# A four-layer graph network on one core: count matrix in bytes, one transfer and one conversion per panel

## What is computed

```
h = relu(layernorm(x)); x = x + spline(h)      # 8 basis weights per edge, segment mean, batch norm, elu
h = relu(layernorm(x)); x = x + gat(h)         # attention: per-edge score, segment softmax, weighted sum
h = relu(layernorm(x)); x = x + gcn3(h)        # three times: agg[dst] += (h@W)[src] * norm, bias, relu
h = relu(layernorm(x)); x = x + sage(h)        # mean of h[src] by dst, joined with h, times W
```

## Time and profile before

| | us |
|---|---|
| median of three timed runs | 11661.3 |
| span of the profiled execution | 9969.6 |
| spline pass, first gather to last | 137 to 3074 |
| GAT pass, first gather to last | 3342 to 6598 |
| four sum passes, first conversion of each | 6737, 7532, 8341, 9157 |
| end of the span | 9970 |

### The profile page before, as it was taken

The page is one execution under the profiler, slowest core; times in us unless marked ns, Lnnn a source line. Parts: engine busy times, 40 slices in busy tenths (PEclk is TensorE's granted clock), DMA queues, the critical chain, the costliest instruction groups (busy, mean ns, idle before and its releaser), DMA issues. The chain is left out here.

```text
span 9969.6 us, 187303 instructions
## 1 busy us (share of the span) xinstructions
PE 7081.0 (71%) x43252; PEld 6159.0 (62%) x43253; DVE 4282.2 (43%) x10967; ACT 4139.5 (42%) x6139; POOL 6744.4 (68%) x6163
## 2 busy tenths in 40 slices
PE   4998888889896466666667777765666766663666
PEld 3998888889895444555555556654554554552555
DVE  6775555555556533333333444452223223224223
ACT  0111111111111233333333444437886885884886
POOL 3667777777775577777777777756655564663663
PEclk9999899999997678878888888878987887996898
DMA  6931111111111333333333333328987996995996
GB/s 244 406 135 17 16 16 16 16 16 16 16 16 5 65 64 64 64 62 64 63 63 62 64 63 64 63 49 250 286 258 219 279 278 186 287 283 161 282 285 195
DMA packets 926246, 1261.57 MB, mean 127 GB/s; under 512 B 326349, under 2 KB 615420, under 8 KB 926075
## 3 DMA queue, kind: packets, MB, share of 16 engines
q1 hardware_dynamic: 403691, 987.27, 29.7%
q0 software_dynamic: 519824, 272.26, 18.0%
q10 hardware_dynamic: 2560, 0.53, 0.0%
HBM read 1052.87 MB, written 206.66 MB: 126 GB/s over the span
## 5 line engine op out<-in xcount | busy, mean ns | idle before, releaser
L561 POOL DMA_INDIRECT gath<-sum_tab,idx_block x1792 | 1788.1, 998 | 1379.4 <-issue 738.0
L837 PE MATMUL psAB<-one_hot,arena 128*128 128x128 f32 x15680 | 2192.7, 299 | 353.5 <-DVE one_hot L1158 352.8
L837 PEld LDWEIGHTS psAB<-one_hot,arena 128*128 128x128 f32 x15680 | 2070.3, 206 | 375.3 <-issue 375.0
L535 POOL DMA_INDIRECT dense<-count_block,cell_block x1120 | 1872.2, 1672 | 524.4 <-issue 329.2
L945 PE MATMUL psCD<-arena_r 128*128 128x512 f32 x5096 | 1513.6, 445 | 642.9 <-ACT arena_r L746 574.1
L561 POOL DMA_INDIRECT gath<-spline_tab,idx_block x1568 | 1512.0, 964 | 632.5 <-issue 417.0
L561 POOL DMA_INDIRECT gath<-gat_tab,idx_block x1568 | 1534.7, 979 | 485.8 <-issue 353.1
L945 PEld LDWEIGHTS psCD<-arena_r 128*128 128x128 f32 x5096 | 1035.9, 214 | 999.2 <-issue 793.7
L746 ACT ACTIVATE arena_r<-stage 128x1792 fp32r<-128x1792 f16 x728 | 1202.8, 1689 | 406.8 <-PE psCD L945 307.4
L1391 DVE SCALAR_TENSOR_TENSOR one_hot<-iota_row,tile_base,dstf 128x512 fp32r<-128x512 f32 x632 | 476.2, 753 | 2043.8 <-PE psAB L931 1724.3
L746 ACT ACTIVATE arena_r<-hT 128x1792 fp32r<-128x1792 f16 x728 | 1199.7, 1687 | 54.7 <-DMA hT<-dense 49.9
(11 more groups left out here) (248 smaller groups left out, 9534.3 us busy)
## 6 DMA issues: line engine op xcount, KB each, us to landing
stage<-dense SPq DMA_DIRECT2D x728, 448.0 KB
hT<-dense SPq DMA_DIRECT2D x728, 448.0 KB
dense<-stage SPq DMA_DIRECT2D x182, 896.0 KB
arena<-dst_rows SPq DMA_DIRECT2D x392, 256.0 KB
gath<-sum_tab,idx_block POOLq DMA_INDIRECT x1792
gath<-spline_tab,idx_block POOLq DMA_INDIRECT x1568
gath<-gat_tab,idx_block POOLq DMA_INDIRECT x1568
sum_tab<-arena_r SPq DMA_DIRECT2D x28, 896.0 KB, 4.7
```

The source lines that it names most:

```text
L535: nc.gpsimd.indirect_dma_start(out=dense, out_offset=bass.IndirectOffsetOnAxis(ap=cell_block[:, c:c + 1], axis=0), in_=count_block[:, c:c ...
L561: nc.gpsimd.indirect_dma_start(out=dest[:, s, j, :], out_offset=None, in_=table, in_offset=bass.IndirectOffsetOnAxis(ap=idx_block[:, c:c + ...
L837: nc.tensor.matmul(block, z[:, w, j, k * P:(k + 1) * P], oh32[:, j, :], start=(j == 0), stop=(j == J - 1))
```

## The change

The matrix is held in bytes (`u8`). A panel of seven tiles is one transfer of 448 KB and one ScalarE conversion of 3584 elements; seven panel buffers take the place of two pairs of halves: two each in `stage`, `hT` and the end of `arena`, one in `early`, an area that held weights and batch norm sums. SyncE loads panel u once panel u - 7 has been turned. Zeroing takes 91 transfers of 896 KB.

Scatters go 41 to a block and begin one iteration earlier (`S0` = 1); 13 are left for the end of the GAT pass.

A byte holds less, so the sources are counted in the GAT pass: in each of the first 35 iterations, for every group, VectorE compares the high and the low part of the source numbers with 0 to 127 (two bf16 operations of 128x512 into `marks`), TensorE multiplies the two one-hots into a 128x128 count in `psE`, and VectorE takes its maximum once per iteration. If a source occurs more than 60 times in one iteration, the matrix is off. `dense_known` is therefore set at the end of the GAT pass and not in the setup, and a quad's sum is multiplied by the flag. SyncE waits for `dense_known` and `scattered` before it stores the first table.

The fp32r product, the gathers and the order of the rounds stay.

```diff
-    SB = 44
-    S0 = 2
+    SB = 41
+    S0 = 1
     NX = 1
-    NY = 20
+    NY = 13
...
-    HC = UC // 2
+    NP = 7
+    CAP = 120
+    LEAD = 4
...
-    JR, JS = 8, 32
+    JR, JS = 16, 64
...
-    dense = nc.dram_tensor("dense", ((NQ * QROWS + JR) * QC, 1), fp16).ap()
+    dense = nc.dram_tensor("dense", ((NQ * QROWS + JR) * QC, 1), u8).ap()
...
+        arena_panels = arena[:, o:o + UC // 2]
...
+        early = sb("early", [P, UC // 4])
+        w_spline, bn = early[:, 0:4 * F], early[:, 4 * F:8 * F]
...
+        src_hi, src_lo = (hT[:, k * DC // 2:(k + 1) * DC // 2].bitcast(bf16) for k in range(2))
+        iota_b = hT[:, DC:DC + P // 2].bitcast(bf16)
+        most = hT[:, DC + P:DC + P + ID]
+        in_tile = stage[:, 0:DC].bitcast(i32)
+        marks = stage[:, 0:2 * GE].bitcast(bf16).rearrange("p (w k j n) -> p w k j n", w=2, k=2, j=J)
...
-        panel = [a[:, h * HC // 2:(h + 1) * HC // 2].bitcast(fp16) for a in (stage, hT) for h in range(2)]
+        panel = [a[:, h * UC // 4:(h + 1) * UC // 4].bitcast(u8) for a in (stage, hT, arena_panels) for h in range(2)]
+        panel += [early[:, :].bitcast(u8)]
...
-            zeros = stage[:, :].bitcast(fp16)
+            zeros = stage[:, :].bitcast(u8)
             sp.dma_start(dense[NQ * QROWS * QC:(NQ * QROWS + JR) * QC, :].rearrange("(p x) o -> p (x o)", p=P),
                          zeros[:, 0:JS]).then_inc(zeroed, 16)
             for q in range(NQ):
-                for u in range(NU):
-                    sp.dma_start(dense_rows[:, q, u * UC:(u + 1) * UC], zeros).then_inc(zeroed, 16)
+                for u in range(NU // 2):
+                    sp.dma_start(dense_rows[:, q, u * 2 * UC:(u + 1) * 2 * UC], zeros).then_inc(zeroed, 16)
...
-            turned = registers(sp, "sp_turned", 2)
+            turned, need = registers(sp, "sp_turned", 2)
 
             def load_panels():
 
                 with sp.Fori(0, NQ) as q:
                     for u in range(NU):
-                        w = u % 2
-                        if w == 0:
-                            sp.reg_add(turned[0], turned[1], 1)
-                            sp.reg_add(turned[1], turned[1], 2)
-                        for h in range(2):
-                            sp.wait_ge(panel_turned[w], turned[h])
-                            sp.sem_inc(panel_free, 1)
-                            at = u * UC + h * HC
-                            sp.dma_start(panel[2 * w + h].unsqueeze(1),
-                                         dense_rows[:, bass.ds(q, 1), at:at + HC]).then_inc(panel_loaded[2 * w + h], 16)
-
+                        sp.reg_add(need, turned, (u + NP) // 2 + 1 + LEAD - NP)
+                        sp.wait_ge(loaded_edges, 16 * 9)
+                        sp.wait_ge(panel_turned[(u + 1) % 2], need)
+                        sp.dma_start(panel[u % NP].unsqueeze(1),
+                                     dense_rows[:, bass.ds(q, 1), u * UC:(u + 1) * UC]).then_inc(panel_loaded[u % NP], 16)
+                    sp.reg_add(turned, turned, NP)
+
+            sp.wait_ge(dense_known, 1)
+            sp.wait_ge(scattered, 16 + 16 * DP)
             with sp.Fori(0, 3) as layer:
                 store_pieces(layer * NS)
-                sp.wait_ge(scattered, 16 + 16 * DP)
...
                 with act.Fori(0, NQ):
                     for u in range(NU):
-                        w = u % 2
+                        w, b = u % 2, u % NP
+                        if b == 0:
+                            act.reg_add(loaded, loaded, 16)
                         if w == 0:
-                            act.reg_add(loaded, loaded, 16)
                             act.reg_add(free, free, 1)
                         act.wait_ge(loaded_edges, 16 * 9)
                         act.wait_ge(panel_used[w], free)
-                        for h in range(2):
-                            act.wait_ge(panel_loaded[2 * w + h], loaded)
-                            nc.scalar.activation(counts[w][:, h * HC:(h + 1) * HC], panel[2 * w + h], ACT.Copy).then_inc(panel_turned[w], 1)
+                        act.wait_ge(panel_loaded[b], loaded)
+                        nc.scalar.activation(counts[w], panel[b], ACT.Copy).then_inc(panel_turned[w], 1)
...
+            def count_sources(i, s):
+
+                pe.wait_ge(marks_ready, i * S + (s + 1))
+                if s == 0:
+                    pe.wait_ge(most_read, i + 1)
+                for j in range(J):
+                    ins = nc.tensor.matmul(psE[:, 0:P], marks[:, s % 2, 0, j, :], marks[:, s % 2, 1, j, :],
+                                           start=(s == 0 and j == 0), stop=(s == S - 1 and j == J - 1))
+                ins.then_inc(marks_used, 1)
+
             pe.wait_ge(visits_init, 2)
-            with pe.Fori(0, IT) as i:
-                group_bounds(pe, i, regs)
-                for s in range(S):
-                    pe.wait_ge(gathered[s], (i + (GAT * IT + 1)) * (16 * J))
-                    with tiles(pe, regs, s):
-                        gat_visit(s)
+            for first, last, counted in ((0, ID, True), (ID, IT, False)):
+                with pe.Fori(first, last) as i:
+                    group_bounds(pe, i, regs)
+                    for s in range(S):
+                        if counted:
+                            count_sources(i, s)
+                        pe.wait_ge(gathered[s], (i + (GAT * IT + 1)) * (16 * J))
+                        with tiles(pe, regs, s):
+                            gat_visit(s)
             with pe.Fori(0, LAG):
...
+            pe.wait_ge(over_known, 1)
+            nc.tensor.matmul(psC[:, 0:4], ones[:, :], over[:, :], start=True, stop=True).then_inc(over_summed, 1)
 
             pe.reg_mov(visit, 0)
 
             first, _ = dense_range(pe, "pe")
             landed, turned, moved, added, pieces = registers(pe, "pe_sum", 5)
-            pe.reg_mov(turned, 2)
...
+            V.tensor_copy(iota_b, iota_row[:, :])
+            link(V.tensor_scalar(in_tile, srci[:, 0:DC], 7, None, ALU.arith_shift_right))
+            link(V.tensor_copy(src_hi, in_tile))
+            link(V.tensor_scalar(in_tile, srci[:, 0:DC], P - 1, None, ALU.bitwise_and))
+            link(V.tensor_copy(src_lo, in_tile))
...
+            def mark_sources(i, s):
+
+                dve.wait_ge(marks_used, i * S + (s + 1))
+                at = bass.ds(i * (S * J) + s * J, J)
+                numbers = iota_b.unsqueeze(1).to_broadcast([P, J, P])
+                V.tensor_tensor(marks[:, s % 2, 0, :, :], numbers, src_hi[:, at].unsqueeze(2).to_broadcast([P, J, P]), ALU.is_equal)
+                V.tensor_tensor(marks[:, s % 2, 1, :, :], numbers, src_lo[:, at].unsqueeze(2).to_broadcast([P, J, P]),
+                                ALU.is_equal).then_inc(marks_ready, 1)
+
+            def read_most(i):
+
+                dve.wait_ge(marks_used, i * S + (S + 2))
+                V.tensor_reduce(most[:, bass.ds(i, 1)], psE[:, 0:P], AX, ALU.max).then_inc(most_read, 1)
+
+            for first, last, counted in ((0, ID, True), (ID, IT, False)):
+                with dve.Fori(first, last) as i:
+                    group_bounds(dve, i, regs)
+                    for s in range(S):
+                        if counted:
+                            mark_sources(i, s)
+                        dve.wait_ge(bc_ready[s % SD], (i * (S // SD) + (s // SD + 1)) * 16)
+                        with tiles(dve, regs, s) as t:
+                            gat_visit(t, dst_bc[:, s % SD, :])
+                        V.engine_nop().then_inc(bc_free[s % SD], 1)
+                        give_back(s)
+                    if counted:
+                        read_most(i)
...
+            link(V.memset(over[:, :], 0.0))
+            link(V.tensor_reduce(over[:, 0:1], most, AX, ALU.max))
+            V.tensor_scalar(over[:, 0:1], over[:, 0:1], CAP // 2 + 0.5, None, ALU.is_ge).then_inc(over_known, 1)
             link(V.reciprocal(s1[:, :], den[:, :]))
             link(V.tensor_tensor(Av, Av, over_features(s1[:, :]), ALU.mult))
+            dve.wait_ge(over_summed, 1)
+            link(V.tensor_scalar(dense_ok[:, :], psC[:, 0:1], 0.0, dense_ok[:, 0:1], ALU.is_equal, ALU.mult))
+            V.tensor_scalar(dense_i[0:1, 0:1], dense_ok[0:1, :], float(ID), None, ALU.mult)
+            V.tensor_scalar(dense_i[0:1, 1:2], dense_ok[0:1, :], float(DB), None, ALU.mult).then_inc(dense_known, 1)
...
-                V.tensor_tensor(at, at, psE[:, 0:QT * F].rearrange("p (t f) -> p t f", f=F),
-                                ALU.add).then_inc(sum_added, 1)
+                V.scalar_tensor_tensor(at, psE[:, 0:QT * F].rearrange("p (t f) -> p t f", f=F), dense_ok[:, 0:1], at,
+                                       ALU.mult, ALU.add).then_inc(sum_added, 1)
```

54 lines of the change are left out of this document (24 added, 30 removed).

## The result

The changed kernel took 11609.95 us (median of 20 runs, 11570.1 to 11646.7) against 11647.1 us (20 runs, 11602.5 to 11676.6) for the kernel before: ratio 0.9969, 95% interval 0.9958 to 0.998, so 37 us faster. The forecast was 98 us. The sign held, and the time lies in the range, which was wide enough to take in the rivals; the size did not hold, and it turns out to depend on the chip.

A forecast was written before the change was run, and what follows sets the result against it. The prediction took GpSimd to pace scatter blocks and the GAT pass, ScalarE the dense quads. Its terms +63 - 84 + 87 + 2 - 166 = -98 us gave 11563 us from 11661.3; range 11420 to 11720, the forecast's own 11490 to 11630.

The forecast's parts named there:

- What bounds the kernel now: Whole kernel: GpSimd paces blocks with scatters and the GAT pass, TensorE blocks without scatters, ScalarE the dense quads.
- slower throughout by 1.17 times: Whole kernel: alternative reading of the 1691.7 us between span and timed median; the gain would then be 115 us.
- schedule term: Spline and GAT passes: 41 scatters per block, starting one iteration earlier, +63 and -84 us, -21 together.
- Zeroing: Start of the spline pass: 91 transfers instead of 182 gain nothing, since the blocks under zeroing are TensorE-bound.
- Scatters: Spline pass +63 us as two blocks become GpSimd-bound; GAT pass -84 us for three fewer scatters in each of 14 blocks.
- Counting: GAT pass: compares hold back GpSimd instructions that start inside them, 0.31 us for each of 280 groups, +87 us.
- Rival A: GAT pass: compares hold GpSimd far oftener, 0.9 us per group, 252 us, so slower at 11728 us; chance 0.13.
- 2.5 us of slack: GAT pass: some 2.5 us per group while TensorE waits for gathers, taken to hide the count's compares and matmuls.
- Dense quads: Sum passes: one transfer and one conversion per panel save 3.2 us in each of 52 quads, -166 us.
- Rival B: Dense quads: TensorE paces, the conversions' gain returns as waits, sum -7, no change at 11654 us; chance 0.15.
- D: Scatters in both passes: adding bytes costs 0.2 us more each, +213, so slower at 11776 us; chance 0.05.
- E: Outside the span: the 1691.7 us shrink with the matrix, up to half of them, some 10800 us; chance 0.04.

The follow-up runs named there:

- e1: The kernel before, unchanged, profiled a second time at the slow pace: 11660.8 us, ratio 1.0013 to the kernel before.
- e2: The changed kernel without the counting of the sources in the GAT pass: 11504.4 us, ratio 0.9882 to the kernel before.
- e4: The changed kernel without the source count and with the old scatter schedule, leaving bytes, single transfer and single conversion: 11433.8 us, ratio 0.9810.
- g1: The changed kernel, unaltered, timed on a chip where the kernel before takes 9967.8 us: 9731.9 us, ratio 0.9763.
- h1: The changed kernel with one counting product per group instead of four, where the kernel before takes 11,661 us: 11580.1 us, ratio 0.9934.
- h2: The changed kernel with a quarter of the compares and all counting products, where the kernel before takes 11,661 us: 11585.7 us, ratio 0.9932.
- e7: The changed kernel with the old scatter schedule and each panel's conversion cut in two halves, at the fast pace: 9814.0 us, ratio 0.9842.
- g4: The changed kernel with the scatter schedule of the kernel before, where the latter takes 9967.8 us: 9763.9 us, ratio 0.9799.
- e3: The changed kernel with the scatter schedule of the kernel before and the count kept, at 11,642 us: 11511.3 us, ratio 0.9876.
- f3: The changed kernel with the source count run in one iteration of 35, where the kernel before takes 11,221 us: 11089.0 us, ratio 0.9891.
- f1: The changed kernel, unaltered, on a chip where the kernel before takes 11,221 us: 11174.6 us, ratio 0.9952.
- e5: The changed kernel with the source count run in one iteration of 35, at the fast pace: 9703.1 us, ratio 0.9731.
- f4: The changed kernel with 53 scatters per block from the fifth iteration on, where the kernel before takes 11,221 us: 11052.4 us, ratio 0.9857.

## Why the prediction was wrong, point by point

**What bounds the kernel now.** Right for the profile and wrong for the runs to be forecast. Page and median stood 1691.7 us apart, and the prediction wrote "No row says what lies in those; I carry them over whole". That is the step that failed. The alternative stood beside it ("slower throughout by 1.17 times") and was drawn as a bare factor on the sum: -115. What the runs showed in its place: the kernel before has a span of 11672 us there (e1), with TensorE slower and GpSimd and ScalarE at their old prices, so each "who paces here" has to be asked anew. Asked so, the schedule term fails: forecast -21, measured +71 (e2 against e4). It makes up more than the whole error of 61 us in the sum; the others are -43 in the bytes (-209 for -166) and +14 in the count (101 for 87). I could have asked it of the rows: TensorE, 154.5 busy of 162 us in a free block, and a total of 11661 that, without time outside the span, is reached only if some engine is slower by hundreds of microseconds.

**Zeroing: 0.** Held. The second spline block, free of scatters, is under zeroing in the kernel before (DMA share 0.99) and past it in the change (0.11), and takes 217 and 213 us at the slow pace:

```profile
349.00:566.00 217.00, 167.86 (x1284) 163.35 (x1285) 117.96 (x260) 20.44 (x58) 107.25 (x114) 0.89 0.99 399
```

```profile
346.00:559.00 213.00, 171.93 (x1293) 168.43 (x1294) 117.09 (x259) 20.44 (x58) 108.58 (x116) 0.87 0.11 25
```

The same rows hold the key to the schedule. At the slow pace a free block takes 213 to 217 us, not 162. GpSimd's own price for a block with 41 scatters, 222 us, is barely above that.

**Scatters: +63 and -84.** At the fast pace +51 and -82; blocks of 222 to 223 us from 460 us on, as forecast. Fast, then slow, a block with 41 scatters each; then slow with 44, the kernel before:

```profile
1126.00:1349.00 223.00, 185.95 (x1452) 183.31 (x1452) 118.60 (x283) 23.21 (x66) 175.17 (x156) 0.90 0.16 17
```

```profile
1087.00:1353.00 266.00, 200.29 (x1450) 193.23 (x1449) 123.73 (x283) 23.22 (x66) 174.94 (x157) 0.83 0.14 14
```

```profile
1006.00:1288.00 282.00, 210.69 (x1450) 200.84 (x1449) 127.06 (x281) 23.21 (x66) 180.08 (x159) 0.81 0.13 13
```

GpSimd is busy the same 175 us in 223 and in 266. A block that gets scatters grows by some 50 us at the slow pace (from 213 to 262), and three scatters fewer take off little. The blocks around the new start of the scatters are 79 us longer together than in e1; the eight behind them are 31 us shorter, of which 20 in the first, and the last four differ by 1 to 3 us each, where three scatters are 5.8 at GpSimd's price. In the GAT pass the 84 us are not there to be had, since GpSimd waits for slots: between 4240 and 7850 us of the change,

```profile
L574 POOL DMA_INDIRECT gath<-gat_tab,idx_block x1565 | 1559.8, 997 | 907.4 <-DVEq L1123 450.8 <-issue 432.5 <-DMA dense<-count_block,cell_block 24.1
```

450.8 us for free slots, against none in the earlier trace rows. Late results are the largest waits here as well; ScalarE's largest wait in the GAT pass of the change, at the slow and then at the fast pace (total us, times, longest):

```profile
ACT arena L725 <- remote: 1123.8, 230, 11.0
```

```profile
ACT arena L725 <- PE psCD L894: 1590.0, 467, 9.1
```

Measured for the schedule: +71 without and +108 with the count, forecast -21.

**Counting: +87.** At the fast pace the mechanism is right and the price three times too high: 29 us. Compares and the GpSimd rows in the GAT pass of g1, then two places:

```profile
L1358 DVE TENSOR_TENSOR stage<-hT 128x512 bf16<-128x512 bf16 x280 | 194.2, 694 | 93.5 <-issue 71.6
...
L574 POOL DMA_INDIRECT gath<-gat_tab,idx_block x1565 | 1543.3, 986 | 483.9 <-issue 353.6 <-DMA dense<-count_block,cell_block 130.1 <-POOL count_block L540 0.2
L548 POOL DMA_INDIRECT dense<-count_block,cell_block x574 | 949.1, 1653 | 200.7 <-issue 168.9 <-DMA dense<-count_block,cell_block 31.7
...
4787.98 0.69 DVE L1358 TENSOR_TENSOR stage<-hT 128x512 bf16<-128x512 bf16 x1
4788.19 1.35 POOL L574 DMA_INDIRECT gath<-gat_tab,idx_block  x1 [0.30 <-issue]
4788.59 0.69 DVE L1359 TENSOR_TENSOR stage<-hT 128x512 bf16<-128x512 bf16 x1
...
4777.36 0.69 DVE L1358 TENSOR_TENSOR stage<-hT 128x512 bf16<-128x512 bf16 x1 [1.59 <-issue]
4777.96 0.95 POOL L574 DMA_INDIRECT gath<-gat_tab,idx_block  x1 [0.30 <-issue]
4777.97 0.71 DVE L1359 TENSOR_TENSOR stage<-hT 128x512 bf16<-128x512 bf16 x1
```

The compare takes 0.69 us (taken: 0.65). The gather that began 0.21 us into a compare ran 0.40 us longer than its usual 0.95, which is about what was left of the first compare; the second did not hold it again, so GpSimd does slip in between the pair. The other gather began 0.01 us ahead of a second compare and lost nothing. GAT blocks with compares took 225 to 230 us, forecast 234. Mean gathers grew from 971 to 986 ns and scatters from 1628 to 1653: 1565 x 0.015 + 574 x 0.025 = 38 us, 0.135 per group, a little under the 0.2 that the prediction held ready for this case; the count cost 29.

The whole trace of g1 bears the two places out. Of the 1519 gathers and scatters recorded in the counted iterations, 254 began inside a compare, and together they ran 34 us longer than the others' mean. All 93 that began between 0.075 and 0.45 us into a compare ran at least 0.1 us longer; of the 31 that began in its first 0.075 us, 23 ran as usual. At the slow pace 259 began inside one, 53 us longer together. Rival A's 0.9 us per group would be 252 us, so it is refuted at either pace as a matter of the lock.

The Trainium skill ("SBUF — State Buffer", on the two sides of SBUF) says that whichever of the two starts first holds the shared ports for its whole instruction, and the other blocks. For GpSimd behind VectorE the 0.40 us agree. The other way round they do not: 238 of the first compares began while GpSimd was in a gather or scatter and took 0.693 us, the other 42 took 0.698; the measurement decides. The rule of its page "VectorE: DVE Perf Modes", that the fast mode of a 16-bit tensor_tensor asks for step 1, agrees with the trace: 694 ns with a repeated column is nowhere near half of the 753 ns of a 512-element one-hot in 32 bits.

At the slow pace the count costs 77 to 101 us. That this is near the forecast's 87 is luck: by h1 and h2 about half of it is TensorE's 1120 products (245 ns each), a cost that the prediction put at nothing, in the "2.5 us of slack", and most of the time appears in the sums (see what stays open). That the slack is gone where TensorE's results come late is argued and not tested.

**Dense quads: -166.** At the fast pace -229 for the whole stage. ScalarE in twelve quads of pass 0, 6815.5 to 7398.4 us, against the earlier trace rows:

```profile
L759 ACT ACTIVATE arena_r<-hT 128x3584 fp32r<-128x3584 uint8 x48 | 150.6, 3182 | 26.6 <-issue 26.6
L759 ACT ACTIVATE arena_r<-arena 128x3584 fp32r<-128x3584 uint8 x48 | 150.5, 3179 | 3.3 <-PE psCD L973 3.0 <-issue 0.3
L759 ACT ACTIVATE arena_r<-stage 128x3584 fp32r<-128x3584 uint8 x48 | 150.4, 3181 | 0.0
L759 ACT ACTIVATE arena_r<-early 128x3584 fp32r<-128x3584 uint8 x24 | 76.3, 3179 | 0.0
L765 ACT ACTIVATE arena<-psCD 128x512 f32<-128x512 f32 x12 | 7.2, 597 | 26.2 <-issue 26.2
```

A conversion takes 3.18 us (forecast 3.19), no wait is put down to a panel, and a quad takes 582.9/12 = 48.6 us (forecast 49.5); the DMA share is 0.68 (forecast near 0.55). Busy time fell by (554.1 - 527.8)/12 = 2.2 per quad (2.1), and ScalarE's idle time as a whole by 1.55 (74.7 us in the earlier trace rows, 56.1 here), about the 1.65 of DMA wait. The two make 3.75, the measured 52.3 - 48.6 = 3.7, so the 0.55 that I let come back as waits did not. (The waits named TensorE fell from 41.0 to 3.0 us, but those called "issue" rose from 12.5 to 53.1, so the names prove little.) That is 192 us for 52 quads. Most of the rest is in the other three passes, whose quads took longer than pass 0's before: from the first conversion of a pass to that of its last quad it was 667, 678, 671 and 677 us, and is 625, 621, 620 and 625. I had sized all 52 from one pass. By e7 against g4, both complete and with the same schedule, (9814.0 - 9763.9)/52 = 1.0 us per quad is what the second launch costs, half of its 2.1 us of busy time (on two chips of the same pace; by the ratios it is 0.8); bytes and panels ahead bring the rest. At the slow pace ScalarE waits longer, 8119 to 8811 us of the change:

```profile
L759 ACT ACTIVATE arena_r<-arena 128x3584 fp32r<-128x3584 uint8 x48 | 151.1, 3183 | 38.2 <-issue 26.1 <-PE psCD L973 8.8 <-remote 3.2
L759 ACT ACTIVATE arena_r<-hT 128x3584 fp32r<-128x3584 uint8 x48 | 151.0, 3184 | 78.6 <-issue 77.7 <-remote 0.5 <-PE psCD L973 0.4
```

yet the term survives there as a whole, -209 by e4 (this includes whatever the sums gain outside the quads).

**The sum.** At the fast pace +51 - 82 + 29 - 229 = -231 for the 236 measured: the forecast of -98 would have been too small there, by 58 for the count, 63 for the quads and 10 for the schedule. At the slow pace -209 + 71 + 101 = -37 for the 37 measured; this adds up by construction, since the terms are steps along one row of kernels from before to change, and says how the 37 divide, not that they had to be so. Rival B (TensorE paces, "-7") named the right engine in the wrong stage; D is excluded by the scatters, in the spline pass of g1 1624 ns each, 1625 in the earlier trace rows; E by e1.

```profile
L548 POOL DMA_INDIRECT dense<-count_block,cell_block x328 | 532.7, 1624 | 99.9 <-issue 99.9
```

**What stays open.** Why TensorE's results come late on some chips; what ran on their other cores is in no trace here. The Trainium skill ("TensorE: Matmul & The Clock Gate", on what can be seen of the gate) tells of a current limiter that slows a whole die once three of its cores run dense matmuls, and of a third clock level by which it shows. No run here shows one: the clock records of all twenty traces have the two levels only. Whether the matmuls or only their results are late there cannot be told from the records. Also open is how the count, done before the sums begin, comes to lengthen them at the slow paces: 3515 us in e2 against 3611 in the change and 3610 in h1, each one execution. It is seen in all three pairs without and with an executed count: 3561 in e4 and 3621 in e3, 3465 in f3 and 3561 in f1; at the fast pace e5 and g1 both have 3005. By the clock records the added time is all at 1.2 GHz (113 us for 95, 73 for 60, 116 for 95). The sums of e2, then of h1:

```profile
7972.00:11487.00 3515.00, 2108.95 (x8922) 1656.95 (x8922) 946.50 (x2110) 2363.23 (x859) 1808.04 (x1811) 0.81 0.53 135
```

```profile
7951.00:11561.00 3610.00, 2148.64 (x8922) 1693.33 (x8922) 946.61 (x2110) 2367.13 (x859) 1799.01 (x1811) 0.80 0.52 131
```

A schedule that is best on every chip was not found: of the complete kernels g1 is the fastest at 9967 us, f4 at 11,221 (f1 the only other), e3 at 11,642 (0.9876, the best complete one there).

## What to carry to other kernels

Before summing terms, hold the span of the profile against the timed median: a gap of 17% meant here that the profile was taken at another pace than the timed runs, and the engine that is slower there must be found before any price is carried over. Price each term under both answers to "who paces this stage"; here the term that only moves work in time (the schedule) changed sign, while the one that removes work (bytes, transfers, launches) kept it. Where two operations share a lock, count only those that start inside the hold.

## What the runs showed of the hardware

- The same program took 9967, 9968, 11221, 11642 and 11661 us on four chips, with mean granted clocks from 0.856 down to 0.794, on a single core. The medians of the one chip met twice agree within 0.2%.
- At the slow pace matmul results arrive late also at a granted clock of 1.00: the read behind a visit's last matmul comes 2.07 us after its modelled end (median of 490 visits; 1.38 at 11,221 us), 0.41 at the fast pace, and 53 to 55 matmuls fit in 8 us where 74 do. The step between matmuls of one line is the same 112 ns.
- ScalarE reads bytes at the price of two-byte and four-byte data (3.18 us for 3584 elements of one byte, 3.19 of two; 32-bit data give the same by the slope of the earlier trace rows, an estimate), and an indirect add of one byte costs GpSimd what one of two bytes costs (1.62 us).
- A VectorE compare of two SBUF operands (0.69 us) holds back a GpSimd gather or scatter that starts 0.075 to 0.45 us into it, in all 93 cases, and not one that is already running: 0.95 us as usual when the compare began 0.01 us later. The compare itself is not held by a gather that is running (0.693 us for 0.698).
